# Window attention in a large fused kernel: the output product with its channels on the partitions, a softmax denominator through ScalarE, and VectorE's search and strip work moved ahead of the output rows

## The reference, cut to what matters

```python
qkv = jnp.einsum('bhwc,cd->bhwd', ln(x), w_qkv) + bias        # rolled by -4, -4, cut into windows of 64 pixels
q = _l2norm(q) * jnp.exp(scale); k = _l2norm(k)
attn = jnp.einsum('bnhqd,bnhkd->bnhqk', q, k) + bias + mask
attn = jax.nn.softmax(attn, axis=-1)
out = jnp.einsum('bnhqk,bnhkd->bnhqd', attn, v)               # per head and window: 64 x 64 by 64 x 16
x = x + jnp.einsum('bhwc,cd->bhwd', out, w_proj) + b_proj
```

## Time and profile before

| | |
|---|---|
| median of 3 runs | 11039.16 us (11031.26 to 11051.44) |
| the profiled execution's own time | 11027.03 us |
| its span, first to last instruction | 11025.2 us |
| busy share of the span | PE 43%, PEld 27%, DVE 51%, ACT 35%, POOL 56% |
| attention stage, first scores read to last (392 steps) | 1076.0 to 3372.0 us |

### The profile page before, as it was taken

One profiled execution on the slowest core, in us unless ns is written; L12 is line 12 of the kernel. 1 busy time (PEld: TensorE's weight loads), 2 busy tenths in 40 slices (PEclk: granted clock), 3 DMA queues, 4 the chain that ended last, 5 costly groups with the idle time before them and its releaser, 6 DMA issues. The chain is left out here.

```text
span 11025.2 us, 125122 instructions
## 1 busy us (share of the span) xinstructions
PE 4769.1 (43%) x29069; PEld 2965.3 (27%) x29069; DVE 5592.9 (51%) x14901; ACT 3867.4 (35%) x9265; POOL 6152.7 (56%) x6259
## 2 busy tenths in 40 slices
PE   0111777777775998784232232232222323323000
PEld 0111666666663554552011011011111101101000
DVE  9997988888886776552121121211211212112477
ACT  0011777777772555332121121121111212212255
POOL 0000444444441221676777777777777777777675
PEclk9755999998996999887666666666666666666555
DMA  0000111111112222553222222222222222222366
GB/s 21 0 0 36 36 32 35 35 32 35 32 35 78 62 61 59 142 147 74 44 47 49 40 51 45 41 51 43 45 48 45 47 44 45 50 40 48 137 237 240
DMA packets 1325844, 659.79 MB, mean 60 GB/s; under 512 B 1058255, under 2 KB 1239100, under 8 KB 1320764
## 3 DMA queue, kind: packets, MB, share of 16 engines
q1 hardware_dynamic: 1142396, 576.49, 19.2%
q0 software_dynamic: 183104, 80.22, 6.2%
HBM read 344.86 MB, written 313.71 MB: 60 GB/s over the span
## 5 line engine op out<-in xcount | busy, mean ns | idle before, releaser
L1843 POOL DMA_INDIRECT gr_rec<-rec,gr_idx x4096 | 3963.3, 968 | 1248.8 <-issue 1247.9
L1864 PE MATMUL gr_p_h<-gr_tT,gr_w 128*128 128x512 f32 x1568 | 848.0, 695 | 3682.3 <-ACT gr_hT L1898 3648.9
L1983 DVE TENSOR_SCALAR gr_pen<-gr_same 128x64 f32<-128x64 f32 x64 | 13.7, 215 | 3170.5 <-DMA gr_rec<-rec,gr_idx 3170.5
L1864 PEld LDWEIGHTS gr_p_h<-gr_tT,gr_w 128*128 128x128 f32 x1568 | 347.0, 226 | 4164.8 <-ACT gr_hT L1898 3734.0
L549 POOL TENSOR_TENSOR at_sq<-at_qk 128x256 f32<-128x256 f32 x392 | 263.9, 673 | 2121.3 <-ACT at_qk L591 2118.9
L1911 ACT ACTIVATE gr_ee<-gr_dd 128x512 f32<-128x512 f32 x64 | 40.3, 629 | 3598.4 <-DVE gr_dd L2002 3598.4
L1869 PE MATMUL gr_p_y<-gr_hT,gr_w 128*128 128x512 f32 x1568 | 688.9, 592 | 0.0
L1963 DVE STREAM_TRANSPOSE gr_z<-gr_yb 128x2048 f32<-128x2048 f32 x98 | 226.5, 2311 | 895.4 <-ACT gr_yb L1903 863.9
L1898 ACT ACTIVATE gr_hT<-gr_p_h,gr_b 128x512 f32<-128x512 f32 x784 | 517.8, 688 | 190.2 <-PE gr_p_h L1864 186.9
L2151 POOL DMA_INDIRECT cb_a<-scan,cb_idx x392 | 503.9, 1286 | 133.7 <-issue 121.1
L1347 POOL DMA_INDIRECT adst<-co_rec,co_idx x448 | 422.8, 944 | 202.5 <-issue 148.5
(11 more groups left out here) (364 smaller groups left out, 13262.2 us busy)
## 6 DMA issues: line engine op xcount, KB each, us to landing
y<-gr_z SPq DMA_DIRECT2D x392, 256.0 KB, 5.2
cb_y<-y SPq DMA_DIRECT2D x28, 3584.0 KB
gr_rec<-rec,gr_idx POOLq DMA_INDIRECT x4096, 2.4
scan<-gr_out SPq DMA_DIRECT2D x64, 768.0 KB, 3.5
at_xs<-in_x_win SPq DMA_DIRECT2D x56, 448.0 KB, 3.9
x<-at_x SPq DMA_DIRECT2D x56, 448.0 KB, 4.5
ff_x<-x SPq DMA_DIRECT2D x56, 448.0 KB, 3.3
x<-ff_x SPq DMA_DIRECT2D x784, 32.0 KB
```

What stands on the lines that cost most here:

```text
L1843: nc.gpsimd.indirect_dma_start(out=rec[s][:, j, :], out_offset=None, in_=rec_dram, in_offset=bass.IndirectOffsetOnAxis(ap=idx[s][:, j:j + ...
L1864: nc.tensor.matmul(p_h[m % 4][:, :], w1[:, P * m:P * (m + 1)], tT[b.k][:, :], start=True, stop=True).then_inc(S["hp"], 1)
```

## The change

The output product is turned round. v is the stationary operand and `pT` is streamed, so that the output comes with 32 channels of two heads on the partitions and the pixels in the columns: `p_O` is 128 x 128 and needs no transpose. A second set of four matmuls with a constant matrix of ones (`heads2`) and `pT` gives the denominators in the same layout. ScalarE turns these into reciprocals as exp(-ln(d)) (`ld`, `rc`), and VectorE multiplies once, straight into `oT`. The reciprocal and product on VectorE, the transpose on TensorE and the copy on ScalarE go. In the same edit ScalarE takes the inverse norms ahead of the copies of q, k, v, VectorE's strip and search work stands between `qkn` and the output rows (`residual` one step later, at j = 3), and `p_den` and `p_xT` share the bank of `p_n`.

```diff
-        vbd = [sb(f"vbd{i}", [P, 2, GRP, VW]) for i in range(PPS)]
+        vbd = [sb(f"vbd{i}", [P, 2, GRP, 2 * HD]) for i in range(PPS)]
...
+        p_den, p_xT = p_n[:, 256:384], p_n[:, 384:512]
...
+        p_O = ps("p_O", [P, P])
...
                         p.wait("rs", 1, 2, 1)
+                        p.wait("den", -2, 2, 1)
+                        p.wait("xT", 3)
                         nc.tensor.matmul(p_n[:, 0:256], same_head[:, :], sq[p.slot(2)][:, :], start=True, stop=True).then_inc(S["norm"], 1)
...
-                        for w in range(2):
-                            for g in range(GRP):
-                                mm = nc.tensor.matmul(p_O[64 * w:64 * w + 64, g, :], pT[r][:, g, 64 * w:64 * w + 64],
-                                                      vb[:, w, g, :], start=True, stop=True)
+                        p.wait("oT", -2)
+                        p.wait("rs", 2, 2, 1)
+                        for g in range(GRP):
+                            rows = slice(32 * g, 32 * g + 32)
+                            for w in range(2):
+                                nc.tensor.matmul(p_O[rows, 64 * w:64 * w + 64], vb[:, w, g, :], pT[r][:, g, 64 * w:64 * w + 64], start=True, stop=True)
+                        for g in range(GRP):
+                            mm = nc.tensor.matmul(p_den[32 * g:32 * g + 32, :], heads2[:, :, :].rearrange("p e c -> p (e c)"), pT[r][:, g, :], start=True, stop=True)
...
-                    if p.has(-2):
-                        p.wait("on", -2, 2)
-                        p.wait("on", -1, 2)
-                        p.wait("xT", 3)
-                        p.wait("oT", -3)
-                        nc.tensor.transpose(p_oT, on[p.slot(-2)][:, :], ident[:, :]).then_inc(S["oTp"], 1)
                     if p.has(4):
                         r = p.slot(4)
                         p.wait("xh", 4)
-                        p.wait("on", -1, 2)
                         p.wait("xT", 3)
-                        p.wait("oT", -3)
+                        p.wait("rs", 2, 2, 1)
+                        p.wait("den", -1, 2, 1)
                         nc.tensor.transpose(p_xT, xh[r][:, :], ident[:, :]).then_inc(S["xTp"], 1)
...
+                    if p.has(-1):
+                        r = p.slot(-1)
+                        p.wait("outp", -1)
+                        nc.scalar.activation(ld[r][:, :], p_den, ACT.Ln).then_inc(S["den"], 1)
+                        p.wait("den", -1, 2, 1)
+                        p.wait("oT", -3)
+                        nc.scalar.activation(rc[r][:, :], ld[r][:, :], ACT.Exp, scale=-1.0).then_inc(S["den"], 1)
...
-                        nc.scalar.activation(oT[p.slot(-2)][:, :], p_oT, ACT.Copy).then_inc(S["oT"], 1)
...
-                        nc.vector.reciprocal(rc[r][:, :].rearrange("p (g e) -> p g e", g=GRP), p_O[:, :, 32:34]).then_inc(S["on"], 1)
...
-                        nc.vector.tensor_tensor(on[r][:, :].rearrange("p (g e c) -> p g e c", g=GRP, e=2),
-                                                p_O[:, :, 0:32].rearrange("p g (e c) -> p g e c", e=2), rr, ALU.mult).then_inc(S["on"], 1)
...
+                    if p.has(-1):
+                        r = p.slot(-1)
+                        p.wait("outp", -1)
+                        p.wait("den", -1, 2)
+                        p.wait("proj", -1 - PPS)
+                        nc.vector.tensor_tensor(oT[(p.u - 1) % PPS][:, :], p_O[:, :], rc[r][:, :], ALU.mult).then_inc(S["oT"], 1)
```

More of the change, by code:

```diff
@@ L379, in attention @@
         pT = [sb(f"pT{i}", [P, GRP, P]) for i in range(2)]
[L380 to L382 removed]
+        ld = [sb(f"ld{i}", [P, P]) for i in range(2)]
+        rc = [sb(f"rc{i}", [P, P]) for i in range(2)]
+        oT = [sb(f"oT{i}", [P, P]) for i in range(PPS)]
+        heads2 = sb("heads2", [P, 2, HD])
         p_s = ps("p_s", [P, GRP, 512])
@@ L582, in emit @@
                         xrstd(0, 0)
+                    if p.has(2):
+                        r = p.slot(2)
+                        p.wait("norm", 2)
+                        nc.scalar.activation(nl[r][:, :], p_n[:, 0:256], ACT.Ln, bias=eps[:, 2:3]).then_inc(S["rs"], 1)
+                        p.wait("rs", 2, 2, 1)
+                        p.wait("qkn", 0)
+                        nc.scalar.activation(rs[r][:, :], nl[r][:, :], ACT.Exp, scale=-0.5).then_inc(S["rs"], 1)
                     if p.has(3):
@@ L737, in emit @@
                         nc.vector.scalar_tensor_tensor(qkn[r][:, :], rs[r][:, :], QK_EPS ** -0.5, qk[r][:, :], ALU.min, ALU.mult).then_inc(S["qkn"], 1)
+                    strip, s, j = p.strip(0)
+                    if j == 1 and p.has(0) and p.has(PPS):
+                        stats(1 - s, strip + 1)
+                    if j == 3 and p.has(0) and p.has(PPS):
+                        residual(1 - s)
+                    if j == 4 and not (p.first and p.u < PPS) and p.u < HALF:
+                        score(1 - s, strip - 1)
+                    if 0 <= p.u < HALF:
+                        k = p.u // PPS
+                        if j == 0 and not (p.first and k == 0):
+                            search.edge_of(v, (p.i, k - 1))
+                        if j == 3:
+                            search.block_of(v, (p.i, k))
+                        if j == 5 and not (p.last and k == 1):
+                            search.partition_of(v, (p.i, k + 1))
+                    if p.has(-1):
[4 more added lines that the diff above has]
+                        nc.vector.tensor_tensor(oT[(p.u - 1) % PPS][:, :], p_O[:, :], rc[r][:, :], ALU.mult).then_inc(S["oT"], 1)
                     if p.has(-3):
@@ L756, in emit @@
                                 score(s, strip)
-                    strip, s, j = p.strip(0)
-                    if j == 1 and p.has(0) and p.has(PPS):
-                        stats(1 - s, strip + 1)
-                    if j == 2 and p.has(0) and p.has(PPS):
-                        residual(1 - s)
-                    if j == 4 and not (p.first and p.u < PPS) and p.u < HALF:
-                        score(1 - s, strip - 1)
-                    if 0 <= p.u < HALF:
-                        k = p.u // PPS
-                        if j == 0 and not (p.first and k == 0):
-                            search.edge_of(v, (p.i, k - 1))
-                        if j == 3:
-                            search.block_of(v, (p.i, k))
-                        if j == 5 and not (p.last and k == 1):
-                            search.partition_of(v, (p.i, k + 1))
                 search.partition_of(v, (0, 0))
```

33 lines of the change are left out of this document (5 added, 28 removed).

## The result

The changed kernel takes 10943.01 us (median of 4 runs, 10921.97 to 10950.05) against 11044.33 of the kernel before on the same chip (4 runs, 11031.26 to 11051.44): a ratio of **0.9907, 95% interval 0.9895 to 0.9918**, 101 us less. The profiled execution has 10950.05 us, 77 less than the one before.

A forecast was written before the change was run, and what follows sets the result against it. VectorE's instruction list in the attention stage was taken as the bound. Instructions -94, waits -52, late reciprocals +7 and squares +19 gave -120 us: 11039 to 10919, forecast bounds 10875 to 10975, stated range 10875 to 11000.

The forecast's parts named there:

- What comes off that list comes off the stage.: Attention stage: VectorE's own instructions set the 5.87 us step, so time cut from them shortens the stage.
- The list, -94: VectorE's instructions: one product replaces reciprocal and product, saving 0.24 us a step over 392 steps, 94 us.
- The waits, -52 + 7: VectorE's waits: 32.5 us before the reciprocal and 19.2 before qkn go; +7 for late rc at the lower clock.
- The squares, +19: GpSimd's squares, some 0.9 us later, overlap VectorE's L712 in one more step of seven: +19 us, bounds 0 and 169.
- Rival (d): Squares fall on VectorE's L712 in most steps, or gathers are late: some +100 us more, near 11020; chance 0.04.
- X = 0.9: TensorE's new output product with denominators takes 0.9 us a step; lower bound 0.45, upper 1.8.
- The ring: ScalarE and TensorE's closed chain of hand-offs: 4.44 us a step, 4.95 at the lower clock, under VectorE's 5.50.
- (a): TensorE's new product runs its column strips one after another and TensorE becomes the bound: +55 us, 11094; chance 0.06.
- (b): Weight loads on TensorE stand open besides, the new product taking 2.4 us: +333 us, 11372; chance 0.02.
- (c): VectorE's new product waits for the reciprocals in the short steps: +90 us, leaving -30, 11009; chance 0.09.
- The rule that speaks against it: TensorE: weight loads overlap running matmuls only where row groups differ, which would make the new product 2.4 us.
- Each names an instruction that ScalarE does earlier in the ring.: TensorE's new waits behind ScalarE's logarithms and norms are each for earlier work; +7 us put for late rc.

The follow-up runs named there:

- e8: Changed kernel with the denominators in the bank of p_O and without TensorE's waits that the shared bank asked for: 10947.07 us, 0.991 of before.
- e1: Changed kernel with GpSimd's squares of q and k computed for 2 of 256 columns: 10895.39 us, 0.9862 of before.
- e5: Changed kernel with ScalarE's inverse norms put back behind its copies of q, k, v: 1.0304 of before.
- e6: Changed kernel with VectorE's strip and search work put back at the end of its step, residual at j = 2: 0.9972 of before.
- e11: Changed kernel with the output product and the denominators computed twice: 10971.8 us, 0.9925 of before.

## Why the prediction was right, and by how much it was off

The median came at 10943, 24 us above the forecast of 10919 and inside its range; the profiled pair gained 77 where the sum said 120. The bound and the two large terms were right. That the total came so near is in part luck, since terms that were missing or mis-sized partly cancel. By the steps:

- **"What comes off that list comes off the stage."** Right. No wait of VectorE above 0.03 us a step is left but the turn of the loop, e8 relieves TensorE without effect, and e1 shortens VectorE's own instructions and the time follows.
- **The list, -94.** From start to start in the whole stage the pair held VectorE 172.5 us and the product holds it 81.0: -91.5.
- **The waits, -52 + 7.** Reciprocal and product: 32.5 to 7.0; `qkn`: 19.2 to 6.8; the turn of the loop 83.1 to 81.6. With 1.5 of a new wait at L755 that makes -38 for the -45 put down. "It stands before three lines only" was a misreading: the wait at L753, 17.4 us, was a fourth, and its fall to 7.9 is 9.5 us that the sum didn't have.
- **The squares, +19: the mis-sized term.** The five groups above grew by 45 us, and e1 lies 50 us below the changed kernel. The prediction named the wrong place: L711's mean went down, 724 to 719 ns, its median stayed at 691. I had looked at one instruction, the one that the trace before showed stretched, and asked how often it would be hit. The squares begin later in the step, by the median 2.22 us after the bias addition where it was 1.63 (0.6 us, not the 0.9 put down), and fall on `xh`, `qkn` and the strip work. -91.5 - 38 + 45 = -84.5, and -94 with L753, against 88 measured between first and last step; the search's small instructions, some of them longer and some shorter by a few us, are not in it. Rival (d) had the mechanism, but not the place, and its price of 100 us beyond the 19 was nearly four times what came.
- **That 45 and 50 are close is no proof.** The 45 is the change of five groups, the 50 all that the squares cost. In the kernel before `xh` was stretched too, but beside GpSimd's gathers: sorted by what GpSimd did at the time, it has 422 ns on average in 217 steps with a gather alone and 339 in 105 with neither. In the changed kernel it has 340 beside gathers and 547 in 117 steps beside the squares. One collision went and another came.
- **X = 0.9.** 0.61 us, nearer the lower bound of 0.45. ScalarE's logarithm has 277 ns (taken 0.37) and its exponential 310 (0.31), and its work grew by 89 us, half of the 172 put down. The ring is shorter than I made it, which is why (a), (b) and (c) didn't come: (c) would have shown 90 us at the product, it shows 7.
- **The rule that speaks against it.** L502's 16 instructions are through in 0.25 us (2001.79 to 2002.04, where L504 begins) with their 16 loads beside them (0.29 us from the same start), all on 128 rows. The rule of the Trainium skill, page "TensorE: Matmul & The Clock Gate", section "Part 3: Packing small matmuls — row/col tiling", by which such loads stand open, would have made X 2.4: the trace disagrees. The same section's figure for column strips gave 0.76, an estimate nearer to 0.61 than my 0.9.
- **"Each names an instruction that ScalarE does earlier in the ring."** This sentence carries more than the sum shows. It is true only because the edit also puts the norms first on ScalarE; e5 says what it is worth, 438 us. I booked that reordering as 19.2 us of waits before `qkn`. Likewise the strip work: "moved, not changed: nothing" holds for its own time, and yet e6 loses 72 us without it, in the very wait at the product that the sum took as nearly gone. Both orders were in the change, so the number came out right, with the reason for it half named.
- **The gathers.** VectorE's waits for them are 0.2 us in the changed kernel, as put. With e1's shorter step they are 17.9, so the room was small.
- **Outside the stage.** 11 us more in one pair of executions, below the 20 that would have contradicted the reading. The runs of one kernel differ by 20 to 28, so nothing is concluded from it.

## What to carry to other kernels

When one engine's list sets the step and another engine gets the work, price the order on the helping engine, not only its total: here the same instructions in another order on ScalarE made 4% of difference, in good part because a shared PSUM bank tied TensorE's product to one of them. A change made of several edits can be a gain of which every edit alone is a loss, so undo them one at a time before calling any of them the cause or free. And when GpSimd's elementwise work moves in time, look up for every VectorE instruction near its new place whether some trace shows its kind stretched, not only for the one that was hit before.

## What the runs showed of the hardware

**Matmuls in separate column strips of 32, with all 128 rows, run side by side in float32, loads hidden.** 16 instructions of 64 columns take 0.25 us and the 8 of 128 columns behind them 0.36; at the rate of four full instructions in 0.45 us the two would take 0.88 each, one after the other. The whole set is 2.9 times as fast as that (1.76 to 0.61), the doubled set of e11 3.1 times (1.14 for two).

**GpSimd's `tensor_tensor` and VectorE hold one another up, and which of them pays depends on who starts first.** In the changed kernel's stage, with VectorE's instructions sorted by whether the squares run at the same time, these are longer beside them: `qkn`, `xh`, the dot product, `residual`, the search's comparison and the subtraction. The bias addition, which reads PSUM, has 693 ns at most over 392 times. Reading SBUF alone is not the mark, though: the row maximum does so, ran beside the squares in 88 steps, and was never stretched:

```profile
L708 DVE TENSOR_REDUCE at_mx<-at_lg x392: 685/686/687, 1076.4 to 3284.6; 128x8 f32<-128x512 f32 x196
```

Where the squares had begun first (36 times), `qkn` took 0.76 us on average; where `qkn` had (64 times), it kept its 0.42 and the squares took 0.82 for their usual 0.62. The Trainium skill, page "SBUF — State Buffer", section "SBUF: two separate sides", says that a GpSimd instruction and a VectorE instruction with two SBUF inputs take a shared pair of ports in turn, whoever starts first keeping it to its end. The trace agrees in kind, by these numbers. It does not agree to the last figure: at 2002.81 `qkn`, waiting to GpSimd's end at 2003.36, would have 0.97, and 0.83 was measured.

**More matmuls can raise the granted clock.** Doubled products (e11) came with 0.96 for 0.91, and a TensorE that waits 480 us for ScalarE (e5) with 0.75. So 0.53 us more on TensorE a step may partly have been paid by faster matmuls elsewhere in it, and a wait on TensorE may cost more than its own length; no run separated the two.
